# Piped attention of a fused four-layer network: query and key rows ordered by parity, dimension and pair, with one transfer of 64 partitions per part instead of two of 32

## The chip, the cores and the metric

One core of a Trainium2 chip runs the whole program. The metric is the device time of one execution in microseconds (us); before the change its median over three runs is 2283.68 us.

## The reference

A network of four layers on x of 8 x 256 x 128, each layer an attention half and a feed-forward half with an adaptive layer norm. The part that this case is about is the attention with 16 heads of dimension 8 in layers 0 and 2, and a second attention inside the feed-forward half of layer 0:

```python
h = _layernorm(x, axis=-1) * (1 + ca) + sa
x = x + ga * _L0_attn_ref(h, ...)      # 16 heads of 8, ALiBi bias, causal softmax
h = _layernorm(x, axis=-1) * (1 + cb) + sb
x = x + gb * _L0_ffn_ref(h, ...)       # latent attention with RoPE, then 4 experts
# inside each attention
scores = jnp.einsum('bhqd,bhkd->bhqk', q, k) / sqrt(8)   # masked where key > query
out = jnp.einsum('bhqk,bhkd->bhqd', softmax(scores), v)
```

Layer 1 (attention with kept keys, then 32 experts of which 4 are picked), the feed-forward half of layer 2 and layer 3 are computed too and lie outside the change.

## The kernel before

Three attentions run as a software pipeline, here called the piped ones: `l0_attn` (batches m = 0 to 7), `l0_ffn` (m = 8 to 15, in the same run of 16) and `l2_attn` (m = 16 to 23). Instead of a float32 matmul with 8 rows, each head's scores are one bf16 matmul with a **stack** of rows. Query and key are split into three bf16 parts (`split_qk`, L942 to L946 on POOL); six pairs of parts (`SLOTS`) of 8 rows each, then bias, mask and maximum rows, make up to 60 rows. Two heads of a pair (the two parities) stand at partitions 0 and 64; the eight pairs lie along the free axis. There are three stacks, batch m uses stack m % 3.

After the projection the 128 rows of query or key are ordered (parity i, half u, dimension d, a), where the pair is 4u + a. `expand_half` (L660) copies them into the stack: for one parity, one half u and one slot, 32 source partitions go to 8 stack partitions x 4 pairs. That is 2 x 12 transfers for a batch (`EXPANDS` = 12), 32 KB each, all issued by SP (SyncE), except that ACT issues the second parity of the first batch of a run.

The order of the work is written out by hand. In iteration m, over six units k = 0 to 5:

- PE computes the turned scores of batch m (L1348) and the scores of batch m + 1 (L1323), adds masks (L1299), weighs the values (L1372) and projects batch m + 3 (L1410 to L1421).
- DVE takes the row maxima of m + 1 (`max_piped`, L2576), and query and key of batch m + 3 into `qk_compact` (`intake_piped`, L2583 and L2584); in l0_ffn it applies RoPE (`keys_ffn`, L2436, for m + 2). It also does the norms (for l0_ffn in advance: `norm_ffn`, L2416 to L2421).
- ACT takes the exponentials (L3812) and issues two small transfers of the maxima for each half (L3823).
- POOL splits the maxima (L928 to L932), takes roots (L918, L964) and splits query and key (`split_qk`); in l2_attn it also issues gathers (L1124), whose results DVE sums (L3300).
- SP waits in `expand_piped` for `parts_split` (L774) and issues the expansion. For l0_ffn's first three batches two transfers that clear the bias rows (L780) go first, after the turned scores of batch m - 3.

PE waits at k = 0 for the first half of the expansion and at k = 3 for the second:

```python
if k % 3 == 0:
    pe.wait_ge(stack_in[u].sem, stack_in[u](m + 1, 0))
```

Ahead of the first iteration ("the front") the first three batches are normed, projected and split. SP loads x, the weights of l0_attn (L730), constants, the staged bias and mask rows (L741 to L746) and then the weights of l0_ffn in three transfers (L726, L727: the RoPE tables, L728: a broadcast bias). PE's `scale_of_ffn` (L1275) needs the l0_ffn weights before it goes on to batch 2. ACT copies the staged rows into stacks 1 and 2 (L3880), DVE into stack 0 (L2656).

Of the kernel before, what the change touches and what calls it, by code (L numbers as in the profile page):

```python
# [12 lines left out]
ACT = mybir.ActivationFunctionType  # L13
AX = mybir.AxisListType

P = 128
# [4 lines left out]
HPG = 2  # L21
# [160 lines left out]
def adaln_program(nc, x_in, c_in, const_in, ali_in, weights_in, out):  # L182
    ctx = ExitStack()
    with ctx:
# [226 lines left out]
        no_bias = tail[0][0:STACK_ROWS, 6144:6272].bitcast(BF16)  # L411
        h_ring = tail[1][:, 0:H_RING * S].rearrange("p (i t d) -> p i t d", t=T, d=D)
# [108 lines left out]
        stack_in = [tally(f"stack_in{u}", 16 * EXPANDS) for u in range(2)]  # L521
# [11 lines left out]
        bias_gone = once("bias_gone")  # L533
# [185 lines left out]
        def _(sp):  # L719
            sp.dma_start(x[:], x_in.rearrange("b (t p) d -> p (b t) d", p=P)).then_inc(x_loaded, 16)  # L720
            def load(i):
                n = DOWN_AT if WEIGHED[i] == "l1_ffn" else places[WEIGHED[i]][1]
                if WEIGHED[i] == "l0_ffn":
# [3 lines left out]
                    sp.dma_start(region[1][:, end:n], weights_in["l0_ffn"][:, end:n]).then_inc(loaded[i], 16)  # L727
# [32 lines left out]
            def expand_piped(ph):  # L760

                first, many = RUNS[ph]
                if ph == "l2_attn":
                    sp.wait_ge(stacks_clear, 8)
# [6 lines left out]
                else:  # L771
                    sp.wait_ge(stacks_clear, 4)
                for m in range(first, first + many):
                    sp.wait_ge(parts_split.sem, parts_split(m, 1))  # L774
                    if B <= m < B + STACKS:

                        sp.wait_ge(turned_psum.sem, turned_psum(m - STACKS, NU))
                        for i in range(HPG):
                            at = 64 * i + STACK_ROWS
                            sp.dma_start(stacks[m % STACKS][at:at + ALI_ROWS, :, 0, :], no_bias).then_inc(bias_gone, 16)  # L780
# [18 lines left out]

            load(1)  # L800
            for i, ph in enumerate(WEIGHED):
                if 1 <= i < len(WEIGHED) - 1:
# [5 lines left out]
                    load(i + 1)  # L808
                if ph in RUNS:
                    expand_piped(ph)  # L810
# [11 lines left out]
        def _(pool):  # L822
# [112 lines left out]
            def split_qk(m):  # L935
# [3 lines left out]
                if place_of(m) >= 2:  # L939
                    for u in range(2):  # L940
# [3414 lines left out]
```

## Time and profile before

| | us |
|---|---|
| device time, median of three runs | 2283.68 |
| the three runs | 2282.6, 2284.66, 2283.68 |
| span of the profiled execution, first to last instruction | 2254.9 |
| PE, DVE, ACT, POOL busy in that span | 1619.9, 1582.2, 1112.7, 1074.0 |
| run of l0_attn and l0_ffn, first row maximum to last | 42 to 418 |
| run of l2_attn, first row maximum to last | 1533 to 1691 |

The profiled execution's span is 2254.9 us; its own device time is not listed beside it, and 28.8 us lie between that span and the median of the runs, outside the first and the last instruction. Times in the profile count from the start of the span. SPq and ACTq are the queues on which SP and ACT issue transfers; the time of a row there is what issuing takes, not the transfer. "issue" is time in which an engine waited for nothing that the profile shows.

### The profile page before, as it was taken

What the parts mean: (1) busy time and instruction counts of PE and PEld (TensorE: products, weight loads), DVE (VectorE), ACT (ScalarE), POOL (GpSimd) and SP (SyncE); (2) the same over time, 40 slices, a digit from 0 to 9 for tenths busy, and PEclk for the clock granted to TensorE, in tenths of its full rate; (3) what the DMA queues carried; (4) which work ended last, traced back from release to release, by engine and by line L of the source; (5) the groups of instructions that cost most, each with busy time, mean ns of one, the idle gap of its engine ahead of it and who ended that gap; (6) DMA issues with size and microseconds to landing.
All of it is one profiled execution on the core that took longest, in us unless ns stands there. A gap on an engine that the chain in (4) does not pass through costs nothing.

```text
span 2254.9 us, 37747 instructions
## 1 busy us (share of the span) xinstructions
PE 1619.9 (72%) x11926; PEld 1177.7 (52%) x11926; DVE 1582.2 (70%) x4925; ACT 1112.7 (49%) x3308; POOL 1074.0 (48%) x1384
## 2 busy tenths in 40 slices
PE   4887888875266857766746966734686889999955
PEld 3444665662155645655646745632343367777742
DVE  6778665445688888888887683245675578888667
ACT  2543444425867776776762322311343266766710
POOL 4433212006184584574565437767521066776711
PEclk7988999985555555555555688965796899999967
DMA  4111000011000000000000102322211000000000
GB/s 135 47 43 43 29 19 28 14 78 40 15 8 8 15 8 8 13 10 8 1 1 1 53 21 86 104 82 70 61 35 72 13 1 1 2 2 1 2 1 19
DMA packets 67302, 67.51 MB, mean 30 GB/s; under 512 B 9955, under 2 KB 58966, under 8 KB 66566
## 3 DMA queue, kind: packets, MB, share of 16 engines
q1 hardware_dynamic: 58930, 53.09, 7.2%
q0 software_dynamic: 5120, 10.50, 1.7%
q8 instruction: 98, 1.61, 0.3%
q10 hardware_dynamic: 3040, 1.38, 0.2%
q14 instruction: 114, 0.93, 0.1%
HBM read 30.41 MB, written 8.39 MB: 17 GB/s over the span
## 4 chain that ended last, share of the span: by engine, by line
DVE 31%; PE 27%; POOL 15%; issue 10%; ACT 10%; SPq 6%; DMA 1%; ACTq 1%; DVEq 0%; POOLq 0%
SPq L660 5%; DVE weights L2963 5%; POOL weights L1116 4%; ACT rope_c L3970 3%; ACT rope_s L3970 3%; PE bank L1510 3%; PE bank L1974 2%; PE bank L1526 2%; PE bank L1695 2%; POOL weights L1124 2%; DVE small L3004 2%; POOL hid L1091 2%; DVE feat_o L3016 2%; PE bank L2105 1%; PE bank L2023 1%
## 5 line engine op out<-in xcount | busy, mean ns | idle before, releaser
L1695 PE MATMUL bank<-V,probsT 128*128 128x9 f32 x1024 | 233.2, 361 | 81.4 <-ACT probsT L3981 81.4
L1695 PEld LDWEIGHTS bank<-V,probsT 128*128 128x128 f32 x1024 | 223.3, 325 | 118.3 <-ACT probsT L3981 99.3
L2576 DVE TENSOR_REDUCE nmax<-bank 128x4 f32<-128x1024 f32 x144 | 175.8, 1221 | 68.0 <-PE bank L1299 61.2
L3981 ACT ACTIVATE probsT<-bank 128x512 f32<-128x512 f32 x128 | 75.9, 596 | 177.7 <-PE bank L1682 175.3
L4122 ACT ACTIVATE big<-bank,nmax 128x256 f32<-128x256 f32 x256 | 119.4, 484 | 51.9 <-DVE nmax L3504 51.9
L860 POOL TENSOR_TENSOR big<-big,rinv 128x512 f32<-128x512 f32 x128 | 132.5, 1050 | 19.1 <-DVE rinv L3510 19.1
L3812 ACT ACTIVATE feat_o<-bank 128x1024 f32<-128x1024 f32 x72 | 73.7, 1023 | 98.2 <-PE bank L1299 65.3
L3812 ACT ACTIVATE O<-bank 128x1024 f32<-128x1024 f32 x72 | 73.7, 1023 | 94.9 <-PE bank L1299 64.1
L1116 POOL DMA_INDIRECT weights<-h_rows,V x96 | 91.1, 948 | 51.2 <-issue 29.0
L2890 DVE TENSOR_REDUCE nmax<-bank 128x2 f32<-128x512 f32 x128 | 85.5, 682 | 42.0 <-PE bank L1669 41.5
L1669 PE MATMUL bank<-qT 48*128 48x256 bf16 x256 | 69.8, 400 | 43.7 <-ACT weights L3924 33.2
L3504 DVE TENSOR_REDUCE nmax<-bank 128x2 f32<-128x512 f32 x128 | 81.8, 680 | 24.6 <-PE bank L1974 24.6
L1682 PE MATMUL bank<-const,big 128*128 128x128 f32 x256 | 61.7, 421 | 36.1 <-POOL big L1099 36.1
L3864 ACT ACTIVATE hid<-bank,weights 128x256 f32<-128x256 f32 x128 | 52.8, 470 | 60.4 <-PE bank L1510 60.4
L3285 DVE TENSOR_TENSOR O<-O,bank 128x512 f32<-128x512 f32 x24 | 16.5, 687 | 90.5 <-ACT O L4045 90.5
L1974 PE MATMUL bank<-kT,qT 32*128 32x256 f32 x1024 | 67.6, 402 | 17.1 <-POOL kT L869 16.6
L3970 ACT ACTIVATE rope_s<-big,small 128x256 bf16<-128x256 f32 x156 | 77.3, 499 | 3.5 <-DVE small L2936 3.5
L1510 PE MATMUL bank<-next_feat,weights 128*128 128x256 f32 x256 | 74.5, 443 | 5.4 <-ACT next_feat L3853 5.4
L3970 ACT ACTIVATE rope_c<-big,small 128x256 bf16<-128x256 f32 x156 | 77.4, 499 | 0.8 <-DVE small L2936 0.7
L1124 POOL DMA_INDIRECT weights<-y_rows,V x64 | 62.0, 968 | 30.5 <-issue 16.3
L1682 PEld LDWEIGHTS bank<-const,big 128*128 128x128 f32 x256 | 52.6, 232 | 42.8 <-POOL big L1099 39.3
L4130 ACT ACTIVATE big<-bank 128x512 f32<-128x512 f32 x128 | 70.5, 617 | 1.9 <-PE bank L2001 1.9
(756 smaller groups left out, 5172.3 us busy)
## 6 DMA issues: line engine op xcount, KB each, us to landing
qT<-parts SPq DMA_DIRECT2D x276, 32.0 KB
big<-V SPq DMA_DIRECT2D x192, 32.0 KB
y_rows<-weights SPq DMA_DIRECT2D x24, 256.0 KB, 2.5
big<-parts SPq DMA_DIRECT2D x180, 32.0 KB
weights<-in_weights_l_ffn SPq DMA_DIRECT2D x1, 4832.0 KB, 15.5
weights<-in_weights_l_attn SPq DMA_DIRECT2D x1, 3904.0 KB, 11.7
qT<-V SPq DMA_DIRECT2D x96, 32.0 KB
weights<-in_weights_l_ffn SPq DMA_DIRECT2D x1, 2860.0 KB, 11.8
```

Source lines behind the costliest of these rows:

```text
L660: queue.dma_start(stacks[m % STACKS][to, u * HALF:(u + 1) * HALF], pair_of(m, at, *of)).then_inc(stack_in[u].sem, 16)
L860: nc.gpsimd.tensor_tensor(row, row, rinv[:, h % H, :].unsqueeze(2).to_broadcast([P, T, S]), ALU.mult).then_inc(scaled.sem, 1)
L1116: nc.gpsimd.indirect_dma_start(gathered[i % RING1][:, t, :], None, h_rows, bass.IndirectOffsetOnAxis(ap=token_of[:, at:at + 1], axis=0)).t ...
L1510: last = mm(pb[2 * (e % 2) + u][:, c * S:(c + 1) * S], W(ph, "w1")[:, at:at + P], next_feat[:], start=True, stop=True)
L1682: last = nc.tensor.transpose(pb[6 + h % 2][:, at], row_of(b, 2 * h + t)[:, k * P:(k + 1) * P], C("ident"))
L1695: last = mm(pb[1][:, t * S + h * wide:t * S + (h + 1) * wide], probsT[:, h % 2, at:at + P], values_of(b, k)[:, h * wide:(h + 1) * wide], s ...
L1974: last = mm(pb[i][:, t * S:(t + 1) * S], queries3[q % 2][of, u, t * P:(t + 1) * P], keys3[q % 2][of, u, :], start=u == 0, stop=u == 1)
L2576: V_.tensor_reduce(to, scored.rearrange("p (i a n) -> p i a n", i=HPG, n=n), AX.X, ALU.max, negate=True).then_inc(score_max.sem, 1)
L2963: link(V_.tensor_scalar(at_most[:, j, :], row_of(b, j), tried[at][:, 0, j:j + 1], 0.0, ALU.is_le, ALU.add, accum_out=tried[at][:, 1, j:j + ...
L3812: nc.scalar.activation(turned_probs[n % TURNS], turned_scores, ACT.Exp).then_inc(turned_exp.sem, 1)
L3970: nc.scalar.activation(signs[signed[0] % len(signs)], row_of(b, j), ACT.Sign, bias=tried[at][:, 0, j:j + 1], scale=-1.0, accum_out=tried[a ...
L4122: last = nc.scalar.activation(probs3[h % PROBS3][:, t * S:(t + 1) * S], pb[h % 4][:, t * S:(t + 1) * S], ACT.Exp, bias=nmax[:, h % H, t:t ...
```

## The change

Query and key rows now have the order (parity i, dimension d, half u, a), so that the 64 rows of a parity read as dimension by pair. One transfer then brings all of a parity's rows for a slot: 64 source partitions to 8 stack partitions x 8 pairs. `expand_half` becomes `expand`, with 12 transfers of 64 KB for a batch. `stack_in` now counts by m % 2 and no longer by half; PE waits once, at k = 0, and SP waits for all six turned units of batch m - 3 before it writes that stack.

The new order has to be in everything that makes those rows. The columns of the query and key weights are copied into the new order by ACT (`weights_of`, 4 copies of 128 x 64 for l0_attn and l2_attn each, 8 for l0_ffn). The bias columns and the RoPE tables are loaded in eight transfers of 16 partitions each (`load_by_parity`) instead of with the rest. In the front, stacks 0, 1 and 2 are staged under semaphores of their own: DVE's intake of batch 0 comes ahead of its copy into stack 0, and ACT's copy into stack 2 comes after the first expansion.

```diff
-        stack_in = [tally(f"stack_in{u}", 16 * EXPANDS) for u in range(2)]
+        stack_in = [once(f"stack_in{u}") for u in range(2)]
+        staged = [(stacks_clear, 2), (x_loaded, 17), (c_loaded, 17)]
...
-        def expand_half(queue, m, u, sides=range(HPG)):
+        def expand(queue, m, sides=range(HPG)):
...
-                    at = slice((2 * i + u) * HD * HALF, (2 * i + u + 1) * HD * HALF)
-                    queue.dma_start(stacks[m % STACKS][to, u * HALF:(u + 1) * HALF], pair_of(m, at, *of)).then_inc(stack_in[u].sem, 16)
+                    at = slice(HD * NG * i, HD * NG * (i + 1))
+                    queue.dma_start(stacks[m % STACKS][to], pair_of(m, at, *of)).then_inc(stack_in[m % 2], 16)
...
+            def load_by_parity(i, first, end, done):
+
+                of = weights_in[WEIGHED[i]][:, first:end].rearrange("(i u d a) n -> i a d u n", i=HPG, u=2, d=HD)
+                for j in range(HPG):
+                    for a in range(HALF):
+                        sp.dma_start(region[i % 2][64 * j + a:64 * (j + 1):HALF, first:end], of[j, a]).then_inc(done, 16)
...
-                    sp.dma_start(region[1][:, end:n], weights_in["l0_ffn"][:, end:n]).then_inc(loaded[i], 16)
+                    load_by_parity(i, end, n, loaded[i])
...
+            load_by_parity(0, *bias_columns(0), biases_loaded)
             load(1)
...
-                    for u in range(2):
-                        if m > first:
-
-                            sp.wait_ge(stack_in[u].sem, stack_in[u](m, 0))
-                        if m >= first + STACKS:
-
-                            sp.wait_ge(turned_psum.sem, turned_psum(m - STACKS, 3 * u + 3))
-                        expand_half(sp, m, u, range(HPG) if m > first else (0,))
+                    if m < STACKS:
+                        sp.wait_ge(*staged[m])
+                    if m >= 2:
+                        sp.wait_ge(stack_in[m % 2], expanded(m - 2))
+                    if m >= first + STACKS:
+
+                        sp.wait_ge(turned_psum.sem, turned_psum(m - STACKS, NU))
+                    expand(sp, m, range(HPG) if m > first else (0,))
...
-                pe.wait_ge(loaded[1], 3 * 16)
+                pe.wait_ge(loaded[1], 10 * 16)
...
-                if k % 3 == 0:
-
-                    pe.wait_ge(stack_in[u].sem, stack_in[u](m + 1, 0))
+                if k == 0:
+
+                    pe.wait_ge(stack_in[m % 2], expanded(m))
...
+                pe.wait_ge(silu_done, 2 if m < B else 3 if m < 2 * B else 4)
+                mm(pb[6][:, 0:S], by_parity(ph, "wq"), f, start=True, stop=True)
...
+                else:
+                    dve.wait_ge(biases_loaded, N_BIASES if m == 0 else N_BIASES_L2)
...
+            def weights_of(ph, i, n):
+
+                act.wait_ge(loaded[i], n)
...
+                        last = nc.scalar.activation(to, W(ph, name)[:, 64 * j:64 * (j + 1)].rearrange("p (u d a) -> p d u a", d=HD, u=2), ACT.Copy)
...
-                expand_half(act, first, 0, (1,))
+                expand(act, first, (1,))
                 if ph == "l0_attn":
                     take_normed(first + 2)
-                expand_half(act, first, 1, (1,))
+                    weights_of("l0_ffn", 1, 10 * 16)
+                    nc.scalar.activation(stacks[2].rearrange("p g side n -> p (g side n)"), staging, ACT.Copy).then_inc(staged[2][0], 1)
```

On SP, from the staging of the bias rows to the first batch, the program before has (names: `big` holds stacks 1 and 2 and the staged rows, `qT` stack 0, `parts` and `V` the split parts, the sizes are those of the destination):

```order
L743 DMA big<-probs 3x8x256 x2
L746 DMA big<-probsT 3x8x512 x2
L726 DMA weights<-in_weights_l_ffn 128x5720
L727 DMA weights<-in_weights_l_ffn 128x1024
L728 DMA weights<-in_weights_l_ffn 128x512
L660 DMA qT<-parts 8x4x512 [waits parts_split,stacks_clear]
L660 DMA qT<-parts 8x8x256 x5
L660 DMA qT<-parts 8x4x512
L660 DMA qT<-parts 8x8x256 x5
```

and the changed one at the same place:

```order
L775 DMA big<-probs 3x8x256 x2
L778 DMA big<-probsT 3x8x512 x2
L742 DMA weights<-in_weights_l_attn 16x1x2 x8
L758 DMA weights<-in_weights_l_ffn 128x5720
L742 DMA weights<-in_weights_l_ffn 16x1x1024 x8
L760 DMA weights<-in_weights_l_ffn 128x512
L667 DMA qT<-parts 8x8x512 [waits stacks_clear,parts_split]
L667 DMA qT<-parts 8x16x256 x5
```

Eight small transfers now stand ahead of the l0_ffn weights, the RoPE tables are eight transfers instead of one, and SP issues 6 expansions for the first batch where it issued 12.

Still on SP, one whole batch (m = 8) before, its clearing of the bias rows included:

```order
L780 DMA big<-weights 6x8x256 x2
L660 DMA big<-parts 8x4x512
L660 DMA big<-parts 8x8x256 x5
L660 DMA big<-parts 8x4x512
L660 DMA big<-parts 8x8x256 x5
L660 DMA big<-parts 8x4x512
L660 DMA big<-parts 8x8x256 x5
L660 DMA big<-parts 8x4x512
L660 DMA big<-parts 8x8x256 x5
```

and in the changed program:

```order
L810 DMA big<-weights 6x8x256 [waits turned_psum,parts_split]
L810 DMA big<-weights 6x8x256
L667 DMA big<-parts 8x8x512 [waits turned_psum,stack_in0]
L667 DMA big<-parts 8x16x256 x5
L667 DMA big<-parts 8x8x512
L667 DMA big<-parts 8x16x256 x5
```

Of the 24 expansions 12 are left, each with twice the rows, and they all stand ahead of the one wait of PE.

## Rows read from the trace of the kernel before

**Rows 1.** The page, part 4: the chain that ended last, by line.

```profile
SPq L660 5%; DVE weights L2963 5%; POOL weights L1116 4%; ACT rope_c L3970 3%; ACT rope_s L3970 3%; PE bank L1510 3%; PE bank L1974 2%; PE bank L1526 2%; PE bank L1695 2%; POOL weights L1124 2%; DVE small L3004 2%; POOL hid L1091 2%; DVE feat_o L3016 2%; PE bank L2105 1%; PE bank L2023 1%
```

**Rows 2.** SP queue in order of time: start us, us, line, transfers.

```profile
9.79 1.21 SPq L726 DMA_DIRECT2D weights<-in_weights_l_ffn  x1
11.05 1.90 SPq L727 DMA_DIRECT2D weights<-in_weights_l_ffn  x1
12.99 0.51 SPq L728 DMA_DIRECT2D weights<-in_weights_l_ffn  x1
...
33.83 17.51 SPq L660 DMA_DIRECT2D big<-V  x24
51.44 17.93 SPq L660 DMA_DIRECT2D big<-parts  x24
...
164.44 1.57 SPq L780 DMA_DIRECT2D big<-weights  x2
166.12 17.79 SPq L660 DMA_DIRECT2D big<-parts  x24
```

**Rows 3.** Chain that ended last, 110 to 240 us: start us, us, what.

```profile
123.11 2.36 DMA big<-V
...
217.13 2.34 issue
```

**Rows 4.** DVE in order of time: row maxima (L2576), norm in advance (L2416).

```profile
55.60 1.22 DVE L2576 TENSOR_REDUCE nmax<-bank 128x4 f32<-128x1024 f32 x1 [1.17 <-PE bank L1299]
...
117.72 1.23 DVE L2576 TENSOR_REDUCE nmax<-bank 128x4 f32<-128x1024 f32 x1 [1.26 <-PE bank L1299]
...
132.99 0.59 DVE L2416 TENSOR_SCALAR weights<-x,small 128x128 f32<-128x128 f32 x2
...
135.81 1.23 DVE L2576 TENSOR_REDUCE nmax<-bank 128x4 f32<-128x1024 f32 x1
...
156.28 1.23 DVE L2576 TENSOR_REDUCE nmax<-bank 128x4 f32<-128x1024 f32 x1
```

**Rows 5.** PE idle ahead of the scores (L1323), 115 to 236 us: us, times.

```profile
  issue: 7.9, 3
  DMA qT<-parts: 1.0, 1
  DMA big<-V: 0.3, 1
```

**Rows 6.** Issuing by line and tile: ns min/median/max.

```profile
L660 SPq DMA_DIRECT2D big<-V x192: 684/685/1360, 33.8 to 1680.3; - x192
...
L780 SPq DMA_DIRECT2D big<-weights x4: 745/764/785, 164.4 to 208.1; - x4
...
L769 SPq DMA_DIRECT2D big<-mask_rows x4: 448/448/449, 1492.7 to 1496.5; - x4
...
L3823 ACTq DMA_DIRECT2D big<-probsT x64: 717/720/802, 65.7 to 1699.8; - x64
```

**Rows 7.** The front: intake of batch 0, first maximum (DVE); scale of l0_ffn (PE).

```profile
19.33 0.48 DVE L2583 TENSOR_SCALAR weights<-bank,weights 128x256 f32<-128x256 f32 x1
...
42.01 1.15 DVE L2576 TENSOR_REDUCE nmax<-bank 128x4 f32<-128x1024 f32 x1
...
27.10 3.75 PE L1275 MATMUL bank<-weights,feat_o 128*128 128x128 f32 x16 [0.28 <-DVE weights L2547]
```

**Rows 8.** Landing of the last l0_ffn load (L728), from its issue.

```profile
DMA to landing us min/median/max: 12.5/12.5/12.5
```

**Rows 9.** The front by stretches: length, PE, PEld, DVE, ACT, POOL, PEclk, DMA share, GB/s.

```profile
10.00:16.00 6.00, 4.85 (x24) 4.49 (x25) 3.55 (x22) 0.56 (x1) 1.75 (x2) 1.00 0.85 234
16.00:22.00 6.00, 1.40 (x6) 0.57 (x4) 4.77 (x11) 4.88 (x2) 1.66 (x2) 0.93 0.91 381
```

**Rows 10.** l2_attn: an expansion (SP) and the first maximum of the same batch (DVE).

```profile
1598.21 17.58 SPq L660 DMA_DIRECT2D big<-parts  x24
...
1624.06 1.22 DVE L2576 TENSOR_REDUCE nmax<-bank 128x4 f32<-128x1024 f32 x1 [0.83 <-PE bank L1299]
```

More of the change, by code:

```diff
@@ L411, in adaln_program @@
         no_bias = tail[0][0:STACK_ROWS, 6144:6272].bitcast(BF16)
+        weights_by_parity = {"l0_attn": (0, {"wq": TAIL + 6272, "wk": TAIL + 6400}), "l2_attn": (0, {"wq": TAIL + 6272, "wk": TAIL + 6400}),
+                             "l0_ffn": (1, {"wq": 8836, "wqr": 8964, "wuk": 9092, "wukr": 9220})}
         h_ring = tail[1][:, 0:H_RING * S].rearrange("p (i t d) -> p i t d", t=T, d=D)
@@ L808, in _ @@
                     load(i + 1)
+                    if WEIGHED[i + 1] == "l2_attn":
+                        load_by_parity(i + 1, *bias_columns(i + 1), biases_loaded)
                 if ph in RUNS:
@@ L939, in split_qk @@
                 if place_of(m) >= 2:
-                    for u in range(2):
-                        pool.wait_ge(stack_in[u].sem, stack_in[u](m - 1, 0))
+                    pool.wait_ge(stack_in[m % 2], expanded(m - 2))
                 link(nc.gpsimd.tensor_copy(part(0), qk_compact))
@@ L951, in prepare_piped @@
                 if ph == "l0_attn":
-                    pool.wait_ge(stacks_clear, 4)
+                    for in_place in staged:
+                        pool.wait_ge(*in_place)
                 for i in range(2):
@@ L2141, in _ @@
             l1_ffn()
-            pe.wait_ge(loaded[4], 16)
+            pe.wait_ge(loaded[4], 2 * 16)
             piped("l2_attn")
@@ L2654, in piped @@
                 if ph == "l0_attn":
+                    intake_piped(first)
                     dve.wait_ge(ali_loaded, 16 * N_STAGED)
-                    V_.tensor_copy(stacks[0].rearrange("p g side n -> p (g side n)"), staging).then_inc(stacks_clear, 1)
-                if ph == "l0_attn":
-                    intake_piped(first)
+                    V_.tensor_copy(stacks[0].rearrange("p g side n -> p (g side n)"), staging).then_inc(staged[0][0], 1)
                     norm_piped(first + 1)
@@ L3872, in take_tokens @@
                 nc.scalar.activation(feat[:], pb[7][:, 0:T * P], ACT.Copy).then_inc(o_feat_n.sem, 1)
+            def weights_of(ph, i, n):
+                act.wait_ge(loaded[i], n)
+                of, (_, at) = places[ph][0], weights_by_parity[ph]
+                for name in at:
+                    for j in range(HPG):
+                        to = by_parity(ph, name)[:, 64 * j:64 * (j + 1)].rearrange("p (d u a) -> p d u a", d=HD, u=2)
+                        last = nc.scalar.activation(to, W(ph, name)[:, 64 * j:64 * (j + 1)].rearrange("p (u d a) -> p d u a", d=HD, u=2), ACT.Copy)
+                last.then_inc(silu_done, 1)
             def piped(ph):
                 first = RUNS[ph][0]
+                weights_of(ph, WEIGHED.index(ph), 2 * 16)
                 take_normed(first)
@@ L3878, in piped @@
                     act.wait_ge(ali_loaded, 16 * N_STAGED)
-                    for st in stacks[1:]:
-                        nc.scalar.activation(st.rearrange("p g side n -> p (g side n)"), staging, ACT.Copy).then_inc(stacks_clear, 1)
+                    nc.scalar.activation(stacks[1].rearrange("p g side n -> p (g side n)"), staging, ACT.Copy).then_inc(staged[1][0], 1)
                 take_normed(first + 1)
                 if ph == "l0_attn":
-                    act.wait_ge(stacks_clear, 4)
+                    act.wait_ge(*staged[0])
                 else:
```

43 lines of the change are left out of this document (28 added, 15 removed).

## The prediction

> **What bounds the kernel now.** I read the chain of work that ended last first. SP's issuing of the expansion (L660) stands at its head, with 5% of the span [rows 1], some 113 us. That looks like the prize, since the change halves the number of these transfers. The next view is SP's own queue. 24 transfers take 17.5 us, and in the early batches they follow each other without a gap [rows 2]. So there are two questions: what do the engines wait for beside that queue, and is it the first twelve transfers or the second twelve that somebody waits for?
>
> The row maxima on DVE give the pace of the batches. The first unit of batch 1 is at 55.60, that of batch 5 at 117.72 [rows 4]: 62.1 us for four batches, 15.5 us each. SP needs 17.5 us a batch, yet it has a lead at the start (its batch 1 begins at 33.83, 22 us ahead of the maximum), and that lead is used up only near batch 5. A chain that is followed back from the end shows SP up to there because SP was never idle. It doesn't show how little earlier the next step could have come. That is in the waits: from 115 to 236 us PE stood idle ahead of the scores for 0.3 us (the landing at 123.11 + 2.36, the last on which the chain goes through SP in this run [rows 3]), 1.0 us, and 7.9 us in three waits [rows 5]. Before 115 us there is none worth a term.
>
> The 1.0 us before the scores of batch 6 is covered. From 132.99 DVE is busy with the norm in advance for l0_ffn, and it reaches the maximum only at 135.81, with no idle time before it [rows 4]. The three waits of 7.9 us are those of batches 8, 9 and 10, the last being the 2.34 us at 217.13 [rows 3]. There the chain runs in a ring: keys, split on POOL, clearing of the bias rows (1.57 us), then twelve expansions, landing, scores, maximum, keys again. For batch 8 the bias rows go at 164.44 and the expansions from 166.12 [rows 2]. PE waits only for the *first* twelve before k = 0.
>
> **The parts of the change.**
>
> *Issuing.* Is a transfer of twice the rows twice as dear to issue? The issue time doesn't follow the number of rows: 685 ns for 32 source partitions (32 KB), 764 ns for the bias rows (6 x 8 runs), 717 ns for ACT's maxima (3 x 4 runs) [rows 6]. The lower bound is 0.69 us, the upper twice that. I take 0.70, by the rows that are nearest in form. SP then needs 12 x 0.73 = 8.8 us a batch with the gaps, instead of 17.5. The halving is real.
>
> *What it frees in l0_attn.* SP is no longer near the pace of 15.5 us, so the 0.3 us goes, and the 1.0 us goes only under DVE's norm: **-0.3**. Bounds: 0 and -1.3. What is late next is DVE and PE themselves. SP now waits for all six turned units of batch m - 3 instead of three. Those end one whole iteration before the scores that need the stack, and 8.8 us plus about 2 us of landing fit into 15.5 us. That wait costs nothing, and its cover is some 4 us.
>
> *What it frees in the ring of batches 8 to 10.* Nothing. Before, PE waited for 12 transfers at k = 0 and for 12 more at k = 3. Now it waits for 12 in all, at k = 0. The count ahead of k = 0 is the same, and each is twice as large. 32 KB more at the 381 GB/s at which the loads ran in the front [rows 9] are 0.09 us; the bounds are 0.09 and 0.5 (the part of the 2.36 us after the issue that can be transfer at all). I take 0.2 us, three times: **+0.6**.
>
> *l2_attn.* The expansion of batch 20 starts at 1598.21 and takes 17.58 us, and the maximum of that batch's first unit is at 1624.06 [rows 10]. The expansion isn't waited for there: with or without its second half it lands in time. 0, with 0.5 as the upper bound for the first batch, where two queues at once move double the bytes.
>
> *The copies of weights.* ACT makes 4, 8 and 4 copies of 128 x 64 ahead of the runs, where it waits for PE and for loads. 0; the cover is ACT's idle time before the first projection. The intake of batch 0 now comes ahead of the stack copy instead of behind it at 19.33 [rows 7], on the same engine and in the same sum: 0.
>
> *The front.* Here the change adds something to a queue that others stand in. Eight small transfers for the bias columns go out ahead of the l0_ffn weights. For their price I have 448 ns (24 runs from DRAM) and 764 ns [rows 6]; I take 0.55 plus a gap of 0.04: 4.7 us. The load that started at 9.79 [rows 2] starts at 14.5. Before, the last of its parts landed at 12.99 + 12.5 = 25.5 [rows 2, 8], and PE needed it at 27.10, when DVE's gates let it start [rows 7]: a slack of 1.6 us. The three parts have 3628 KB. At 381 GB/s they take 9.5 us, with 2.4 us of landing 11.9 us; as they ran before, partly at 234 GB/s [rows 9], they took 15.7 us. So they land between 26.4 and 30.2, and PE, DVE and the first maximum at 42.01 [rows 7] come 0 to 3.1 us later (4.7 with the dearer issue). I take **+1.4**, nearer the fast end, because the slow stretch from 10 to 16 us is the one shared with the staging transfers, which now have those 4.7 us for themselves. Splitting the l0_attn load puts the constants back by one issue, at most 0.43 us: **+0.3**.
>
> The RoPE tables go in eight transfers of 16 partitions, 0.55 us each, against one of 1.90 us [rows 2]. SP is done with them near 22 us and is needed at about that time. By rows alone their bytes cost nothing more. The Trainium skill speaks against them (DMA: Bandwidth & Descriptors, "Why a DMA increments its semaphore by 16 and not by 1"): a transfer issued by SP runs on the largest number of engines up to 16 that divides the slowest dimension of both sides, which for 8 row groups against 16 partitions is 8, where a load of 128 partitions has 16. By that rule the 512 KB of tables would take 2.8 us instead of 1.4 us at the rate above, an estimate, and the sum would be 1.4 us higher. No row before shows it.
>
> **The sum.** -0.3 + 0.6 + 1.4 + 0.3 = +2.0 us. The profiled execution has a span of 2254.9 us and 28.8 us around it to the median of the runs, 2283.7, which the change doesn't touch. So 2285.7 us. 0.2%, about what a measurement of this kernel can tell from no change, is 4.6 us. The forecast is therefore: no difference.
>
> **The rivals.**
>
> *Faster, because SP's queue held the whole first run.* For it: SP's issuing is the chain's largest entry among transfers [rows 1], and the chain leaves it only at the landing at 123.11 [rows 3]. If all batches up to 7 had the pace of 15.5 us, the first maximum of batch 7 would come at 55.6 + 6 x 15.5 = 148.6 instead of 156.28 [rows 4], and the run would gain over 7 us: 2276. Against it: PE's waits [rows 5] are 1.3 us where this would need 7, and DVE's extra norm at 132.99 [rows 4] explains the longer period.
>
> *Slower, through the front.* The eight bias transfers cost 0.8 us each, the tables come late, and the load lands at 32 to 33 us, 5 to 6 us after PE wants it. Everything behind shifts by that much. It decides against the change from a landing later than about 30.5 us. With the other terms: +6.5, 2290. For it: DMA is busy to 0.85 and 0.91 in that time [rows 9], so a later start is a later landing. Against it: the slack of 1.6 us and the staging that goes ahead.
>
> *Slower, because the transfer doesn't do what it says.* If issuing a transfer of 64 partitions costs 1.37 us, SP is as slow as before, and PE at k = 0 waits for all of it. Batches 8 to 10 wait 8 us longer each: +25, 2311. The rows on issuing speak against it.
>
> **Chances.** No difference, 0.58: 2279 to 2288. Faster rival, 0.12; another 0.05 for small shifts of when TensorE's clock falls to half, which I can't work out and which go either way. Slower through the front, 0.20. Dear issuing, 0.05. That makes faster 0.17, same 0.58, slower 0.25. The range goes from 2278 to 2291: it takes in the bounds of the front and most of the first rival, and leaves out the dear issue and the full gain of that rival.
>
> **What would show it right or wrong.** SP's expansion lines: 12 a batch at 0.69 to 0.72 us, about 8.8 us, and long idle stretches between them. The chain: L660's successor falls to about 2 or 3%, and PE, DVE and ACT take its place in the first run at the same pace, about 15.5 us from maximum to maximum. PE's waits ahead of the scores of batches 8, 9 and 10 stay at 2 to 4 us each. The front: the first l0_ffn load goes out near 14.5, the last part lands near 28.5, and the first maximum is at 43 to 44 instead of 42.01. The forecast is wrong if the pace of batches 1 to 4 falls clearly below 15 us, if those three waits shrink, or if the first maximum comes later than 46 us.

## The result and the profile after

The changed kernel takes 2333.14 us (median of 4 runs, 2328.62 to 2340.62) against 2284.17 us before in the same measurement: ratio 1.0212, 95% interval 1.0193 to 1.0231. It is 49 us slower, clear of the noise, and the interval lies on both sides of 2%. The forecast was no difference, 2285.7, with 2291 as the upper end: the time is outside the range, and above even the dearest rival, 2311.

The page of the changed kernel: the line on the transfers issued by SP (packets, MB, share of 16 engines' time) and the page's size of a transfer; then SP's queue in one batch of l0_attn, the first four of its twelve transfers:

```profile
q1 hardware_dynamic: 57442, 53.08, 10.4%
...
big<-parts SPq DMA_DIRECT2D x90, 64.0 KB
...
87.39 2.64 SPq L667 DMA_DIRECT2D big<-parts  x4
```

The same line of the page of before:

```profile
q1 hardware_dynamic: 58930, 53.09, 7.2%
```

SP's part is as forecast: 12 transfers of 64 KB in 8.0 us. But the transfers' own time is 10.4% of 16 engines, where it was 7.2% for the same 53 MB. The bytes are the same; they move more slowly.

The first profile of before came from a quicker execution than its timed runs (span 2254.9), so its span can't be taken from the 2326.8 of this one. The 28.8 us between that span and the median of the runs don't lie outside the first and the last instruction, as the text ahead of the prediction has it: in the profiles whose own device time is known the two differ by 1.7 to 1.9 us (2251.22 and 2249.5 for the kernel before). I profiled both kernels again on one chip: spans 2249.5 and 2307.3, ratio of that measurement 1.0219 (1.0200 to 1.0239), medians 2258.48 and 2308.41. From here on "before" and "after" are these two. Cut at DVE's first row maximum of a batch, the 57.8 us between the spans lie here (the third column is an experiment below):

| stretch, us | before | after | strided_rows |
|---|---|---|---|
| front, to the first maximum of batch 0 | 40.8 | 46.0 | 45.8 |
| batch 0 to batch 7 | 113.4 | 116.8 | 111.2 |
| batch 7 to batch 10 (the ring) | 64.2 | 76.2 | 62.4 |
| batch 10 to batch 15 | 184.3 | 189.2 | 185.1 |
| batch 15 to 16 (layer 1, start of l2_attn) | 1126.0 | 1137.3 | 1130.1 |
| batch 16 to 23 (l2_attn) | 144.4 | 163.3 | 146.3 |
| batch 23 to the end | 576.4 | 578.5 | 577.6 |

The two large entries are the ring, +12.0, and l2_attn, +18.9. I had +0.6 and 0 for them. The first two traces show them as well, +11.6 and +19.8. The small ones are less firm: the front is +2.9 there instead of +5.2, and batch 10 to 15 is -0.2 instead of +4.9. What PE waited for ahead of the scores between 110 and 240 us (us, times), before and then after (where [rows 5] showed 7.9 us in three waits):

```profile
  issue: 7.8, 3
```

```profile
  issue: 18.9, 3
```

The same three waits, 11.1 us longer. PE waits there at k = 0 for the landing. So when does it land? The DMA view of one expansion of l0_attn in the changed kernel, from 87 to 104 us: the mean busy share of the engines and the GB/s in 40 slices of 0.425 us, then packets and shares.

```profile
88.33 1.98 SPq L667 DMA_DIRECT2D big<-parts  x3
...
DMA  0000004243656665686665565666666665200000
GB/s 0 0 0 0 0 0 99 78 117 75 71 59 61 51 74 47 53 111 49 71 59 46 87 51 67 72 55 75 52 75 63 63 69 43 25 1 14 0 14 0
...
q1 hardware_dynamic: 1504, 0.79, 40.9%
```

SP has issued the last transfer at 96.4. The bytes flow on until 101.5, mostly at 50 to 75 GB/s, with the engines busy to five or six tenths. Before, 24 transfers of half the size kept them busy to one or two tenths (12.6% over 162 to 186 us). The page's issue lines can't show this. Its queue line hints at it, and the DMA view shows it.

### The profile page after: what moved, and what is told of

It reads as the page before. It is cut to its first block and busy times, and to the rows that moved or that the text cites. A ratio compares the mean times of both kernels' runs of the same rounds, so it can differ in the third digit from the quotient of the medians.

```text
span 2326.8 us, 37473 instructions
## 1 busy us (share of the span) xinstructions
PE 1630.7 (70%) x11926; PEld 1183.1 (51%) x11926; DVE 1584.4 (68%) x4925; ACT 1113.6 (48%) x3324; POOL 1078.6 (46%) x1384
## 3 DMA queue, kind: packets, MB, share of 16 engines
q1 hardware_dynamic: 57442, 53.08, 10.4%
## 5 line engine op out<-in xcount | busy, mean ns | idle before, releaser
L1157 POOL DMA_INDIRECT weights<-y_rows,V x64 | 62.4, 976 | 38.0 <-DMA y_rows<-weights 18.2
```

## The experiments

Three theories were open after that. **T1**: the 8 neighbouring partitions of the stack that each transfer writes take bytes only at a certain rate. Before, 32 KB each 0.73 us (45 GB/s) stayed below it; 64 KB each 0.66 us (99 GB/s) do not. **T2**: reading 64 source partitions in one transfer is slow. **T3**: transfers that are in flight at once disturb each other wherever they go.

### strided_rows and again_before, again_after

The order of the 48 part rows within a stack is free, as long as query and key follow the same one. One line makes the 8 rows of a slot lie six apart:

```diff
-                    to = slice(64 * i + HD * slot, 64 * i + HD * slot + HD)
+                    to = slice(64 * i + slot, 64 * i + STACK_ROWS, len(SLOTS))
```

> The changed kernel with the stack's 48 rows ordered by dimension and slot instead of slot and dimension, so that a transfer writes 8 partitions six apart instead of 8 neighbouring ones. Same rows, same bytes, same number of transfers. Theory T1 (the neighbouring 8 destination partitions take the bytes too slowly; transfers of 64 KB pile up): packets of 512 B fall from a mean of 76 ns to about 30, the last packet comes about 1 us after the last issue instead of 4 to 8, the three waits of batches 8 to 10 lose 4 us each, and the time falls by 12 us in the first run and by up to 20 in l2_attn: near 2300 or less, ratio to before about 1.005. Theory T2 (reading 64 source partitions at this pace is what is slow): no change against the changed kernel, 1.021. Theory T3 (transfers in flight at once disturb each other, wherever they go): no change, 1.021.

> The kernel before itself, profiled on the same chip as the others of this call. Its profiled execution (span 2254.9) lies 27 us under its runs. If that is a matter of the chip and not of the change, the experts of layer 1 (1369 to 1465 us in the first trace, 34 us longer in the changed kernel) are longer here too, and the span is about 2282. If the 34 us belong to the change, this trace is as short there as the first one. Every theory: ratio 1.000.

> The changed kernel itself, profiled on the same chip. Every theory: ratio 1.021, the last packet of each expansion 4 to 8 us after the last issue. Against the trace of before of this call it shows which stretches are longer: about 3 us in the front, 14 in the first run, 20 in l2_attn, and the rest in layer 1.

Measured: strided_rows 2262.02 us, ratio 1.0026 (1.0012 to 1.0039); again_before 0.9993 (0.9981 to 1.0005); again_after 1.0219 (1.0200 to 1.0239). So one line without a change to any byte count takes 1.9 of the 2.2% away. The same view of the same batch in strided_rows:

```profile
87.86 2.63 SPq L667 DMA_DIRECT2D big<-parts  x4
...
DMA  0000042433433425244334340000000000000100
GB/s 0 0 0 0 0 120 65 114 90 92 124 90 88 123 64 160 53 117 125 82 104 120 77 108 0 0 0 0 0 0 0 0 14 8 6 0 0 39 0 0
...
q1 hardware_dynamic: 1504, 0.79, 17.9%
```

The bytes stop at 97.2, 1.3 us after the last issue, and the share of the engines' time falls from 40.9 to 17.9% for the same 1504 packets. PE's waits ahead of the scores:

```profile
  issue: 3.4, 3
```

3.4 us instead of 18.9, and less than the 7.8 of before. In the table, the ring returns to below its value of before and l2_attn to within 2 us of it. T2 and T3 expected nothing of this edit. They fall as the cause.

The expectation for again_before held in neither form as a whole. Layer 1 is as short in this trace as in the first one (1126.0 and 1128.0 us in the table's stretch), which was to mean that the 34 us belong to the change. But on one chip only 11.3 are left of the 34 us by which this stretch differed between the first two traces. The changed kernel itself has 1162.4 us there in its first trace and 1137.3 in its second. The chips of the first two aren't on record; that they differed is the likely reading, since the same 27 to 29 us separate two chips further on.

l2_attn was lost by the same cause in three ways. DVE's longest waits from shortly ahead of its first row maximum on (us, times, longest), in before, after and strided_rows:

```profile
DVE nmax L2576 <- PE bank L1299: 28.3, 30, 5.1
DVE hid L3300 <- DMA weights<-y_rows,V: 12.4, 4, 6.5
```

```profile
DVE nmax L2610 <- PE bank L1332: 38.5, 30, 11.0
DVE hid L3335 <- DMA weights<-y_rows,V: 29.0, 4, 9.9
```

```profile
DVE nmax L2610 <- PE bank L1332: 26.6, 27, 5.6
DVE hid L3335 <- DMA weights<-y_rows,V: 17.1, 4, 6.3
```

First, PE's one long wait for a stack there, that of the first batch (L1323, L1356), in before, after and strided_rows:

```profile
  DMA big<-parts: 7.6, 1
```

```profile
  DMA big<-parts: 13.5, 1
```

```profile
  DMA big<-parts: 8.1, 1
```

These 6.0 us lie ahead of the first row maximum, so they are in the table's stretch 15 to 16; they are also most of the +10.2 us in the line of the maxima. Second, behind the first maximum the sums of the gathered rows (L3335) wait 16.6 us longer for POOL's gathers, which are on another queue and touch no stack. The gathers' packets take 158 ns instead of 132 (the queue's share of 16 engines over its packets). That they are held up because they share the DMA engines with the slow transfers is my reading; no run gave them engines of their own. Third, ACT's small transfers of the maxima come late. PE waits for them ahead of the turned scores (L1381), in l0_attn (46 to 162.8 us) and in l2_attn (1565.4 to 1728.8) of the changed kernel:

```profile
  DMA big<-probsT: 4.5, 3
```

```profile
  DMA big<-probsT: 3.0, 2
  DMA qT<-probsT: 2.7, 1
```

Before and in strided_rows PE has no such wait in either. The 4.5 us fit l0_attn's +3.4. With the rows apart the wait for the gathers is 17.1 us, against 12.4 before.

### probes

Behind the last store, bursts of transfers, each burst waited for before the next starts. The same source and stack rows as in the change:

```diff
+            many([(st[rows_at(i, s)], pair_of(0, all64(i), *SLOTS[s])) for i, s in every])
+            many([(st[rows_by(i, s)], pair_of(0, all64(i), *SLOTS[s])) for i, s in every])
...
+            many([(st[rows_at(i, s), :, 1, :], parts_n[0][all64(i), PARTS + SLOTS[s][1], :]) for i, s in every])
+            many([(stacks[j][rows_at(0, s)], pair_of(0, all64(0), *SLOTS[s])) for s in (0, 4) for j in range(3)])
...
+            many([(st[all64(i), s], pair_of(0, all64(i), *SLOTS[s])) for i, s in every])
+            many([(st[rows_at(i, s)], pair_of(0, all64(i), *SLOTS[s])) for i, s in crossed])
...
```

> The changed kernel with bursts of transfers behind its last store, each burst waited for before the next. Length from first issue to last landing, by T1 / T2 / T3. a, 12 as in the change (64 rows to 8 neighbouring partitions, 64 KB): 13 us by all. b, the same to 8 partitions six apart: 9.5 / 13 / 13. c, 24 of 32 rows as before: 18.5 by all. d, 12 from 64 rows with the key part alone, 32 KB: 9.5 / over 11 / over 11. e, 6 to rows 0 to 7 and 32 to 39 of the three stacks: 7 by T1, or more if neighbouring transfers to the same partitions add up. f, 6 to rows 0, 6, ... and 4, 10, ... of the three stacks: 5.5 / 7 / 7. g, 12 from 64 partitions to 64 partitions, 1 KB a row: 9.5 / 13 / 13. h, as a with the parities by turns: 13 by all, less if what is full is one group of partitions. i, three as in a, one at a time: 2.3 us each by T3, 2.7 by T1. j, three as in b, one at a time: as i by T2 and T3, shorter by T1.

| burst | bytes | us | expected by T1 |
|---|---|---|---|
| a, 12 to 8 neighbouring partitions | 768 KB | 15.2 | 13 |
| b, 12 to 8 partitions six apart | 768 KB | 9.6 | 9.5 |
| c, 24 of 32 rows, neighbouring | 768 KB | 19.2 | 18.5 |
| d, 12 of 64 rows, key part alone, neighbouring | 384 KB | 9.6 | 9.5 |
| e, 6 to rows 0 to 7 and 32 to 39 | 384 KB | 9.7 | 7 or more |
| f, 6 to rows 0, 6, ... and 4, 10, ... | 384 KB | 5.7 | 5.5 |
| g, 12 from 64 partitions to 64 | 768 KB | 9.3 | 9.5 |
| h, as a, parities by turns | 768 KB | 15.2 | 13 or less |
| i, three as in a, one at a time | 64 KB | 2.9 to 3.0 each | 2.7 |
| j, as b, one at a time | 64 KB | 2.3 each | less than i |

Bursts a and b in the DMA view (40 slices each, of 0.38 and 0.24 us):

```profile
DMA  0002424465665666666655665666666666650000
GB/s 0 0 0 51 119 63 111 90 59 53 70 51 59 63 49 62 65 47 69 65 49 65 65 53 74 50 49 77 49 49 77 49 46 78 53 39 7 0 0 0
...
q1 hardware_dynamic: 1504, 0.79, 48.1%
...
DMA  0000044134344244252352432442523524424300
GB/s 0 0 0 0 0 90 128 56 87 111 94 94 130 62 115 111 79 141 71 92 130 79 107 124 51 113 113 75 134 73 100 132 60 113 124 56 119 111 4 0
...
q1 hardware_dynamic: 1504, 0.79, 31.8%
```

b is decisive against T2 and T3: the same 64 source rows and the same bytes as a, only the destination differs, and SP's 7.9 us of issuing bound it. d agrees: 64 source rows, neighbouring destination, but 32 KB each, and nothing piles up. g says it from the other side: 64 rows read, 64 KB, spread over 64 destination partitions, fast. i speaks against T3 too: a transfer that is quite alone takes 0.7 us longer to neighbouring partitions. So it is the destination and the rate. I worked the rate out in three ways. Burst a begins to flow at 2302.3 and stops at 2314.8: 786 kB in 12.5 us, 63 GB/s; b, worked out alike, has 99 GB/s, which is what SP issues. Burst e goes to rows 0 to 7 and 32 to 39 only, 393 kB in 6.9 us: 57 GB/s. And the one transfer of i has its data in 1.2 us if its landing after the last byte takes what j's takes: 55 GB/s, an estimate. The packets of i don't show it: they flow for the same 0.6 us and take the same 32 ns each as j's, and only the landing comes later. A single transfer's packets look fast even where its destination is slow.

The Trainium skill has this as a rule (SBUF — State Buffer, "Door 1: The DMA port swizzle"): the partitions hang on 16 ports of some 27 GB/s, four neighbours (and the four 32 further on) on one, so 8 neighbours reach two ports, about 54 GB/s. By that rule a transfer of 64 KB needs 1.2 us, an estimate; the probes' 55 and 57 GB/s agree. The rule speaks against this change, and I didn't weigh it in the prediction.

One thing stays open. In burst a successive transfers go to different slots, in h even to the other parity by turns, so that the partitions that fill change with every transfer. My expectation had h below a if one group of partitions were what is full. It isn't: both take 15.2 us, at 63 GB/s hardly more than e's 57. It is as if successive transfers of one queue hardly overlapped and each paid for its own few partitions; no run shows why. For the same reason e doesn't test whether rows 32 to 39 share anything with rows 0 to 7: other rows in turn didn't help either.

### before_strided

```diff
-                    to = slice(64 * i + HD * slot, 64 * i + HD * slot + HD)
+                    to = slice(64 * i + slot, 64 * i + STACK_ROWS, len(SLOTS))
```

in `expand_half` of the kernel before.

> The kernel before, its 24 transfers of 32 rows each now written to 8 partitions six apart. T1 (8 neighbouring partitions take about 54 to 64 GB/s, and only transfers that come faster than that pile up): before, 32 KB every 0.73 us are 45 GB/s, its packets take 29 ns and its last packet comes 0.9 us after the last issue, so nothing changes: ratio 0.999 to 1.001. If the order of the rows helps by itself (in another way than by the rate of the transfers), it helps here too: 0.995 or less.

Measured 2253.56 us, ratio 0.9983 (0.9968 to 0.9997). A gain of 0.17% where T1 in my form had at most 0.1%; the interval reaches to that. PE's three waits of the ring are 6.0 us in its trace instead of 7.8, and the ring is 1.1 us shorter. A possible reason: at burst e's 57 GB/s one transfer of 32 KB takes 0.57 us (an estimate), so that its last bytes land later in rows side by side even when transfers come at 45 GB/s. The traces don't place the rest of the 4 us: the two spans are 2249.7 and 2249.5.

### The front: copy_first and act_loads

strided_rows still has a front that is 5.0 us longer. copy_first moves DVE's copy into stack 0 back ahead of the intake of batch 0:

```diff
-                    intake_piped(first)
                     dve.wait_ge(ali_loaded, 16 * N_STAGED)
                     V_.tensor_copy(stacks[0].rearrange("p g side n -> p (g side n)"), staging).then_inc(staged[0][0], 1)
+                    intake_piped(first)
```

> strided_rows with one line moved: DVE copies the staged rows into stack 0 ahead of the intake of batch 0 again, as in the kernel before. Theory F1 (the move took the 2.3 us copy out of DVE's idle time and put it ahead of the next norm, where it also runs beside POOL's split): the second norm comes at about 20.3 instead of 22.4, the first row maximum at 42.5 instead of 45.8, and the time falls by 3 us, ratio 1.0026 - 0.0014 = 1.001. Theory F2 (the front is late because of the loads that go out 7 us later): the first row maximum stays at 45.8 and the ratio at 1.0026.

Measured 2263.47 us, 1.0020 (1.0007 to 1.0033). Three rows of DVE and PE in strided_rows (the copy, the second norm; PE's `scale_of_ffn`), then the same in copy_first:

```profile
20.24 2.28 DVE L2693 CAST qT<-big 128x4096 bf16<-128x4096 f32 x1
22.43 1.86 DVE L2563 TENSOR_SCALAR xb<-x,small 128x128 f32<-128x128 f32 x2
...
31.07 3.76 PE L1308 MATMUL bank<-weights,feat_o 128*128 128x128 f32 x16 [3.29 <-DVE weights L2581]
```

```profile
13.99 2.29 DVE L2692 CAST qT<-big 128x4096 bf16<-128x4096 f32 x1
...
19.28 0.88 DVE L2563 TENSOR_SCALAR xb<-x,small 128x128 f32<-128x128 f32 x2
...
30.20 3.78 PE L1308 MATMUL bank<-weights,feat_o 128*128 128x128 f32 x16 [6.55 <-DMA weights<-in_weights_l_ffn]
```

Both theories were half right. The copy did delay DVE as F1 says. In its new place it came out of DVE's idle time: from the intake (19.45 and 18.49 us) to the norm are 3.0 us in strided_rows and 0.8 in copy_first. POOL's first cast of the split, which ran beside it, takes 2.60 us in strided_rows and 0.66 in copy_first. But when the copy is put back, PE waits 6.55 us for the weights of l0_ffn, which F2 named, and the first maximum only goes from 45.8 to 45.1. That difference is smaller than what one front differs by between traces: bias_first, below, has the same front as copy_first and its first maximum at 47.8, with PE's granted clock at 0.81 there instead of 0.99. So what removing the copy alone is worth in time isn't shown. The waits show that two late things lay side by side. act_loads takes the second away too, by giving the sixteen small loads to ACT's queue:

```diff
-            load_by_parity(0, *bias_columns(0), biases_loaded)
...
+                        act.dma_start(region[WEIGHED.index(ph) % 2][64 * j + a:64 * (j + 1):HALF, first:end], of[j, a]).then_inc(done, 16)
```

> copy_first with the sixteen small loads of the front (eight for the bias columns, eight for the RoPE tables) issued by ACT, which is idle from 2 to 10 us and from 11 to 16 us there, instead of by SP. In copy_first PE waits 6.5 us for the weights of l0_ffn and goes on at 30.20 where the kernel before goes on at 25.9. If the front is late because of these loads once the copy is out of the way, the last of them lands before 27, PE goes on at 26 to 27, the first row maximum comes at 41 to 42 instead of 45.1, and the ratio falls from 1.002 to 1.000 or 1.0005. Rival: the sixteen transfers delay the loads of SP as much from another queue, or hold back ACT's own work ahead of PE's first projection: the first row maximum stays at 44 or more, no change.

Measured 2285.82 us beside 2287.06 us of before (another chip), ratio 1.0000 (0.9987 to 1.0012). PE in its front:

```profile
28.04 3.75 PE L1306 MATMUL bank<-weights,feat_o 128*128 128x128 f32 x16 [2.62 <-DVE weights L2579]
```

It waits for DVE again and no longer for the load, and the first maximum is at 42.9, nearer to the 41 to 42 expected than to the rival's 44. On the same chip best_new, with this front, has 42.0 and best_old, with the front of before, 41.7. With these two edits and the rows apart the change is what I forecast for the change as such: no difference.

### The ring: bias_first, by_part, best_new, best_old

bias_first lets SP clear the bias rows of batches 8 to 10 before it waits for the split parts:

```diff
-                    sp.wait_ge(parts_split.sem, parts_split(m, 1))
                     if B <= m < B + STACKS:
                         sp.wait_ge(turned_psum.sem, turned_psum(m - STACKS, NU))
+                        if m > B:
+                            sp.wait_ge(bias_gone.sem, no_bias_of(m - 1))
...
+                    sp.wait_ge(parts_split.sem, parts_split(m, 1))
```

> copy_first with SP clearing the bias rows of batches 8 to 10 before it waits for the split parts, not after. If these batches run in the ring split, bias rows, expansion, landing, scores, each of the three loses the 1.6 us of the two issues: periods 20.8 to 19.2, time 4.8 us less, ratio 0.999. Rival: PE or DVE takes over as the bound there (l0_attn's own pace is 15.1 us): less, but not less than 0. If the ring is not what bounds them: no change against copy_first.

by_part starts the transfers of each part as soon as POOL has cast it:

```diff
-                    expand(sp, m, range(HPG) if m > first else (0,))
+                    for n, slots in enumerate(((0,), (1, 3, 4), (2, 5))):
+                        sp.wait_ge(parts_split.sem, parts_split(m, n + 1))
+                        expand(sp, m, range(HPG) if m > first else (0,), slots)
```

> bias_first with the expansion started part by part: POOL signals after each of the three casts, and SP issues the 2 transfers that need the first part alone, then the 6 that need the second, then the 4 that need the third. Ring theory: SP starts 3.8 us earlier and only the last 4 transfers (2.6 us) stand behind the last cast if its 8 us of issuing fit; periods of batches 8 to 10 fall by 3.5 to 4 us each to about 15.5, time 10 us less than bias_first, ratio 0.994 to 0.995. l2_attn gains up to 2 us. Rival: the three batches are then bound by something else at 18 us or more: 0.997.

Measured: bias_first 1.0005 (0.9989 to 1.0020), by_part 1.0011 (0.9998 to 1.0023), against 1.0020 of copy_first. PE's waits ahead of the scores of these batches are 4.4 us in copy_first, 1.2 in bias_first and none in by_part. Yet by_part's time isn't below bias_first's, where I expected 10 us. The stretches from batch 7 to 10 and from 10 to 15 (length; PE, PEld, DVE, ACT, POOL busy; PEclk, DMA share, GB/s), of copy_first and of by_part:

```profile
156.40:218.80 62.40, 52.95 (x631) 29.88 (x629) 51.03 (x151) 25.47 (x40) 25.90 (x55) 0.77 0.17 43
218.80:403.90 185.10, 159.19 (x1566) 117.69 (x1566) 111.05 (x359) 79.46 (x150) 43.46 (x96) 0.92 0.10 27
```

```profile
155.90:214.50 58.60, 52.01 (x650) 29.74 (x648) 50.76 (x151) 26.71 (x40) 25.31 (x54) 0.82 0.18 45
214.50:402.20 187.70, 161.16 (x1554) 118.75 (x1546) 111.00 (x360) 78.30 (x149) 43.88 (x96) 0.89 0.10 26
```

The ring itself gained 3.8 us, a quarter of the 15 that I expected of both edits. PE and DVE are then busy 52.0 and 50.8 of 58.6 us, at 19 to 20 us a batch: the rival that one of them takes over fits. And the stretch behind it lost 2.6: PE does the same work with more busy time, 161.2 instead of 159.2 us, at a granted clock of 0.89 instead of 0.92. It looks as if what was gained by idling less were paid back at the lower clock, and all four traces with a shortened ring have 0.88 to 0.90 behind it. But the same stretch differs as much between traces in which the ring is as it was. The changed kernel has it in its first trace (not shown) at 0.92 and 184.0 us, and in its second as

```profile
238.90:428.10 189.20, 165.46 (x1566) 121.58 (x1566) 111.13 (x359) 79.10 (x150) 41.94 (x90) 0.88 0.19 26
```

and act_loads, with copy_first's ring, has 0.89 and 187.5 us. So the length of the stretch goes with the clock, but that the shorter ring caused the lower clock isn't shown, nor which activity sets it.

best_new is by_part with the loads of act_loads; best_old is before_strided with the order of bias_first:

```diff
-                    sp.wait_ge(parts_split.sem, parts_split(m, 1))
                     if B <= m < B + STACKS:
...
+                        if m > B:
+                            sp.wait_ge(bias_gone, 16 * HPG * (m - B))
...
+                    sp.wait_ge(parts_split.sem, parts_split(m, 1))
```

> by_part with the loads of act_loads. If the parts add up: by_part's 1.0011 less 0.0016, that is 0.9995. If what ends the waits of PE is given back by TensorE's clock, as between bias_first and by_part: 0.999 to 1.001 all the same. A version that beats the kernel before by 0.5% is no longer expected from this side.

> before_strided (0.9983) with SP clearing the bias rows ahead of its wait for the split parts, as in bias_first. It has the cheap front of the kernel before and its expansion in halves. If the three waits of 7.8 us in all lose 1.5 us each: 4 us less, 0.9965. If TensorE's clock gives part of it back: 0.9975. Rival: before_strided's gain was chance, then 0.998 to 0.9995.

Measured: best_new 2282.94 us beside 2287.06, ratio 0.9988 (0.9979 to 0.9997); best_old 2285.77, 0.9989 (0.9979 to 1.0000). best_new is the fastest of the kernels that build on the change and faster than both kernels, by 0.12% against before; before_strided, one line on the kernel before, has 0.9983, and the intervals of the three overlap. best_old's ratio is no better than before_strided's, against the 4 us that I expected, though its waits ahead of the scores are down to 0.4 us of "issue" and its ring to 61.6 us from 63.1: the stretch behind it is 4 us longer in its trace, at a clock of 0.88.

## Why the prediction was wrong

- **Issuing**: right in kind. A transfer of twice the rows costs 0.62 us to issue; I took 0.70. The halving is real, and the rival of dear issuing is out.
- **What it frees in l0_attn**: -0.3 was forecast, with -1.3 as the bound. In strided_rows, where the transfers don't pile up, batch 0 to 7 takes 2.2 us less than before: more than my bound, and far from the rival's gain of 7 us, so SP's 5% of the chain were no prize. In the changed kernel the same stretch is 3.4 us longer, with 4.5 us of PE's waits for ACT's transfers of the maxima.
- **What it frees in the ring**: this is the step that failed. "32 KB more at the 381 GB/s at which the loads ran in the front are 0.09 us; the bounds are 0.09 and 0.5." Measured: 12.0 us over three batches, 4.0 each, where I took 0.2; PE's three waits grew from 7.8 to 18.9 us. The count of transfers ahead of k = 0 was right. The price of a byte was from the wrong row: 381 GB/s is the rate of loads into 128 partitions. The nearest row was the expansion itself, 24 times 32 KB in 17.5 us [rows 2], 45 GB/s into 8 partitions, and nothing in the trace had shown it faster. The upper bound was wrong too. It priced one transfer alone, while twelve in a row add their lateness: the last bytes came about 5 us behind the last issue instead of 1. With the rows apart, at the same count and bytes, the waits are 3.4 us: what failed is the price of the bytes, and not the reading of who waits for what.
- **l2_attn**: the same step failed here, with a second one, that the other transfers in flight cost nothing. 0 was forecast, with 0.5 as the bound for the first batch. That batch's expansion alone came 6.0 us later (in the 11.3 us of the stretch ahead). Behind the first maximum 18.9 us were measured, though "the expansion isn't waited for there" held to the end: PE has no wait for a stack after the first batch. I looked at SP's and PE's waits for the expansion and not at the other transfers in flight: the gathers (16.6 us of DVE's waits) and ACT's maxima (5.7 us of PE's).
- **The front**: +1.7 was forecast and +2.9 and +5.2 measured in two pairs of traces. The eight bias loads cost 0.87 us each (6.9 us) where I took 0.59, so the first l0_ffn load went out at 16.8 instead of 14.5. It did land late (with the copy out of the way PE goes on at 30.20, the dear end of my 26.4 to 30.2). What I had at 0, the intake ahead of the stack copy "in the same sum", delayed DVE by 2.2 us: the sum on DVE was the same, but the copy had stood in a gap in which DVE waited for PE, and came to stand ahead of work that was wanted. The rival of a slow front had the right sign and price and was right for 3 to 5 of 50 us: luck in the sign, since the rest of the slowdown has another cause.
- **The rule cited** in the prediction (the Trainium skill, DMA: Bandwidth & Descriptors, "Why a DMA increments its semaphore by 16 and not by 1"), that a transfer from SP runs on 8 engines for 8 row groups, would have added 1.4 us to the tables' load, an estimate. No run here separates it: the sixteen small loads were moved, not widened.
- **The 28.8 us** around the span were a misreading (they are 1.7 to 1.9), without harm to the number, since they were only added to reach the median again.
- **The signs** that I gave of a wrong forecast looked the wrong way: the pace of batches 1 to 4 didn't fall (15.7 us), and I named waits that shrink, not waits that grow. Only the line that the waits stay at 2 to 4 us each caught it: they are 6.3. The first maximum, at 46.0, stood just at its limit.
- **Not settled**: layer 1 with the start of l2_attn takes 1128.4 to 1130.1 us in the four traces with the rows apart on the two quick chips (strided_rows, copy_first, bias_first, by_part) and 1126.0 and 1123.7 us in the two of the old expansion there (again_before, before_strided), though none of layer 1's code changed. In l2_attn's stretch strided_rows keeps 1.9 of the 18.9 us, where DVE's wait for the gathers keeps 4.7.

## What to carry to other kernels

Price a transfer by where its bytes go, not by its size alone: how many destination partitions, how close together, how many bytes per us in a burst. If a change raises the rate at which transfers go to few partitions each, the rate that the trace of before shows there is the only one that is known to be free; a faster one has to be measured, or the rows laid apart, which may cost one line. And while transfers drain slowly the other queues' transfers come late too (here the gathers and the maxima), so look at those before you call a late landing harmless.

Before you move work on an engine "in the same sum", look at whether it stood in a gap. When two things are late side by side, removing one can show next to nothing in the time; look at the waits. And before you explain a few microseconds of one stretch, look at how much that stretch differs between two traces of the same code.

## What the runs showed of the hardware

- Transfers within SBUF to 8 neighbouring partitions each ran at 57 to 63 GB/s (57 in burst e with the same two groups of rows, 63 in a and h with changing ones); transfers to 8 partitions six apart ran at 99 GB/s, as fast as they were issued (9.6 us for a burst whose issuing takes 7.9), without a sign of a limit.
- A slow destination shows as slower packets: by the DMA view, 48.1% of 16 engines over 15.2 us for 1504 packets is 78 ns of engine time a packet in burst a, 31.8% over 9.6 us 32 ns in burst b, and 13.8% over 19.2 us for 1600 packets 27 ns in burst c. In burst a the share rises over the first 2 us and then stays: the slowness builds up with what is already on its way. One transfer alone has 32 ns a packet to either destination (i and j); its landing is 0.7 us later.
- Issuing a transfer of 64 source partitions and 64 KB cost SP 0.62 us, one of 32 and 32 KB 0.69 us.
- DVE's copy of 128 x 4096 beside POOL's cast of 128 x 512: the cast took 2.60 us in the three traces in which the two met in the front (after, again_after, strided_rows), 0.66 where they didn't (again_before, copy_first).
- Two of the three chips of the experiments agree for the kernel before (2258.48 and 2257.76 us), the third is 1.3% slower (2287.06), and 27 to 29 us of it lie in layer 1, by three pairs of traces (before_strided and best_old, copy_first and act_loads, by_part and best_new). Spans of traces from two chips can't be subtracted.
